# Normalizing and turning the attention heads by matmuls with diagonal blocks, in a fused linear-attention and ternary feed-forward kernel

## What is computed

```python
    S = S * jnp.exp(gt)[..., None, None]
    v_new = vt - jnp.einsum('bhk,bhkv->bhv', kt, S)
    S = S + bt[..., None, None] * (kt[..., :, None] * v_new[..., None, :])
    o = jnp.einsum('bhk,bhkv->bhv', qt, S)
...
var = jnp.mean(jnp.square(o.astype(jnp.float32)), axis=-1, keepdims=True)
o = o * jax.lax.rsqrt(var + NORM_EPS).astype(o.dtype) * norm_w
gate = (x @ Wg.T).reshape(B, T, H, DV)
o = o * jax.nn.silu(gate)
return o.reshape(B, T, H * DV) @ Wo.T
```

## Time and profile before

| what | value |
|---|---|
| median of 3 runs | 407.44 us (406.19 to 407.88) |
| the profiled execution: its time, its span | 409.17 us, 407.3 us |
| mean granted TensorE clock | 0.792 |
| DVE busy | 304.1 us, 75% |
| PE busy | 259.5 us, 64% |
| ACT busy | 119.9 us, 29% |
| chain that ended last | DVE 50%, PE 24%, issue 7%, ACT 4% |

### The profile page before, as it was taken

One profiled execution on the slowest core, in us unless ns is written; L12 is line 12 of the kernel. 1 busy time (PEld: TensorE's weight loads), 2 busy tenths in 40 slices (PEclk: granted clock), 3 DMA queues, 4 the chain that ended last, 5 costly groups with the idle time before them and its releaser, 6 DMA issues.

```text
span 407.3 us, 13992 instructions
## 1 busy us (share of the span) xinstructions
PE 259.5 (64%) x6314; PEld 177.6 (44%) x6314; DVE 304.1 (75%) x774; ACT 119.9 (29%) x245; POOL 32.5 (8%) x44
## 2 busy tenths in 40 slices
PE   3993650489558649696567659684484285986541
PEld 1492430445445417364443345353453264655321
DVE  0664898928689995949798987678899955438996
ACT  0783411046722210265413113347022001132010
POOL 2000110002201000011210000013010001010000
PEclk9965585569968868989689589897897595998686
DMA  8500000000000020000000030000000230001001
GB/s 242 208 0 2 2 2 0 3 3 3 3 2 3 3 51 3 2 3 2 3 3 2 4 103 3 2 3 2 4 3 2 63 96 2 3 3 53 2 1 52
DMA packets 8011, 9.65 MB, mean 24 GB/s; under 512 B 1808, under 2 KB 7056, under 8 KB 7952
## 3 DMA queue, kind: packets, MB, share of 16 engines
q1 hardware_dynamic: 7024, 8.41, 6.3%
q10 hardware_dynamic: 928, 0.36, 0.4%
HBM read 6.67 MB, written 2.10 MB: 22 GB/s over the span
## 4 chain that ended last, share of the span: by engine, by line
DVE 50%; PE 24%; issue 7%; ACT 4%; DVEq 0%
PE pc L329 6%; DVE conv_buf L894 4%; PE pj L342 4%; PE pg L450 3%; DVE inv L994 3%; DVE sub_buf L992 3%; PE fr L329 3%; PE fr L473 2%; PE pj L450 2%; DVE stats L1085 2%; DVE r_sb L1033 2%; DVE r_all L882 2%; DVE t_all L881 2%; DVE conv_buf L1079 2%; DVE t_all L880 2%
## 5 line engine op out<-in xcount | busy, mean ns | idle before, releaser
L894 DVE SCALAR_TENSOR_TENSOR conv_buf<-raw,wconv,conv_buf 128x512 f32<-128x512 f32 x72 | 57.6, 806 | 16.7 <-ACT conv_buf L616 15.0
L342 PE MATMUL pj<-xt,wproj 128*128 128x512 f32 x96 | 55.6, 718 | 7.8 <-DMA xt<-x_t 7.1
L684 ACT ACTIVATE u_sb<-pc 128x192 f32<-128x192 f32 x32 | 10.5, 328 | 107.2 <-PE pc L329 107.2
L329 PE MATMUL pc<-r_sb,t_t 32*32 32x64 f32 x672 | 17.1, 237 | 34.3 <-DVE r_sb L1033 33.5
L846 POOL TENSOR_TENSOR s_dec<-s_sb,decay 128x192 f32<-128x192 f32 x24 | 15.8, 660 | 282.5 <-DVE s_sb L1042 153.6
L342 PEld LDWEIGHTS pj<-xt,wproj 128*128 128x128 f32 x96 | 20.0, 228 | 27.6 <-issue 24.1
L329 PEld LDWEIGHTS pc<-r_sb,t_t 32*32 32x32 f32 x672 | 12.0, 115 | 44.8 <-DVE r_sb L1033 44.2
L329 PE MATMUL fr<-x_t,x 32*32 32x16 f32 x768 | 11.8, 210 | 30.5 <-DVE x_t L999 15.8
L329 PEld LDWEIGHTS fr<-x_t,x 32*32 32x32 f32 x768 | 11.2, 151 | 32.1 <-issue 32.1
L450 PE MATMUL pg<-wout,conv_buf 128*128 128x256 f32 x36 | 13.4, 547 | 17.9 <-DVE conv_buf L1079 17.9
L354 PE MATMUL pg<-xt,wproj 128*128 128x512 f32 x48 | 24.1, 624 | 0.0
(11 more groups left out here) (161 smaller groups left out, 534.3 us busy)
## 6 DMA issues: line engine op xcount, KB each, us to landing
xt<-x_t SPq DMA_DIRECT2D x1, 1536.0 KB, 9.1
x_buf<-x SPq DMA_DIRECT2D x3, 512.0 KB, 3.8
out<-hid_buf SPq DMA_DIRECT2D x6, 256.0 KB, 2.2
wproj<-w_proj SPq DMA_DIRECT2D x1, 1024.0 KB, 7.8
xt<-x_t SPq DMA_DIRECT2D x1, 512.0 KB, 5.8
kq<-x SPq DMA_DIRECT2D x1, 512.0 KB, 3.6
out<-v_tok SPq DMA_DIRECT2D x2, 256.0 KB, 2.1
wout<-w_out SPq DMA_DIRECT2D x1, 384.0 KB, 9.9
```

The source lines that it names most:

```text
L329: mm = pe.matmul(out[rows], stationary[rows], moving[rows], **flags)
L342: mm = pe.matmul(pj[:, j % 2, :], wproj[:, t, j * P:(j + 1) * P], xt[:, t, k * TOK:(k + 1) * TOK], start=(t == 0), stop=(t == KT - 1))
L684: act.activation(u_sb[:, :, :].rearrange("p g v -> p (g v)"), pc[:, 0:G3 * DV], ACT.Copy).then_inc(u_done, 1)
L894: e = dve.scalar_tensor_tensor(out=conv[:, d, :, :], in0=raw[:, d, :, m:m + T], scalar=wconv[:, j, m:m + 1], in1=conv[:, d, :, :], op0=ALU ...
```

## The change

- A constant `C_EYE` is added, a 32x32 identity repeated in each 32-row group.
- `head_norm` no longer scales `o_all` and no longer transposes. One DVE instruction writes `r_diag`, 24 diagonal 32x32 blocks with the reciprocal roots on the diagonal (128x768).
- PE's new `heads_to_channels(k)` stands after `merge(k + 1)`. For groups 0 and 1 it issues 2 x 2 x 8 calls of `by_head` (128 matmuls), for group 2 another 64 matmuls that go to off-diagonal blocks of the array. The results lie in four PSUM banks.
- `gated` reads them from PSUM, with four instructions in place of three, and waits for `turn_mm` in three steps.
- `project(k + 2, 0)` and ACT's `tile_out_of_psum(k + 2, 0)` move ahead of the junction's `merge`; the three taps of `conv_taps(…, 0)` move between the instructions of `gated`, for turns 0 and 1.
- `normalize` of the tail moves ahead of `gated`.
- `load_residual` waits for `r_diag_done` in place of `on_scaled`.

```diff
@@ constants
-C_UPPER, C_ROWA, C_ROWB, C_LESS_B, C_END = 644, 676, 677, 678, 679
+C_UPPER, C_ROWA, C_ROWB, C_LESS_B, C_EYE, C_END = 644, 676, 677, 678, 679, 711
...
+        r_diag = view(sub_buf, 0, U, CH)
...
+        head_bank = (pc[:, :], po[:, :], fr[:, 1, 0:T], pg[:, 0:T])
@@ SP
             def load_residual(k):
-                after(sp, on_scaled, 1, k, 1)
+                after(sp, r_diag_done, 1, k, 1)
@@ PE
+            def heads_to_channels(k):
+                after(pe, r_diag_done, 1, k, 1)
+                for h in range(2):
+                    for g in range(2):
+                        for c in range(NC):
+                            t = g * T + c * CH
+                            mm = by_head(head_bank[h][:, t:t + CH], o_all[:, g, c, h * 32:(h + 1) * 32],
+                                         r_diag[:, g * NC + c, :], start=True, stop=True)
+                    mm.then_inc(turn_mm, 1)
+                for c in range(NC):
+                    for h in range(2):
+                        for q in range(4):
+                            rows, at = slice(32 * q, 32 * q + 32), 64 * h + 32 * (q % 2)
+                            mm = pe.matmul(head_bank[2 + q // 2][at:at + 32, c * CH:(c + 1) * CH], o_all[rows, 2, c, h * 32:(h + 1) * 32],
+                                           r_diag[rows, 2 * NC + c, :], start=True, stop=True)
+                mm.then_inc(turn_mm, 1)
...
             def turn(k, front, tail):
-                if front and not first(k):
-                    project(k + 1, 0)
...
                 if front:
+                    if not last(k + 1):
+                        project(k + 2, 0)
                     merge(k + 1)
+                    heads_to_channels(k)
@@ ACT
                 merge_out(k)
-                if front and not first(k):
-                    tile_out_of_psum(k + 1, 0)
...
-                    after(act, on_done, 0, k, 1)
+                    after(act, turn_mm, 0, k, GATE_TILES)
...
                     o_square(k, front)
+                    if not last(k + 1):
+                        tile_out_of_psum(k + 2, 0)
@@ DVE
             def handoff(k, front, tail):
...
-                if front:
+                if front and first(k):
                     conv_taps(k + 1, 0)
...
-                units = o_all[:, :, :, :].rearrange("p g c v -> p (g c) v")
-                dve.tensor_tensor(units, units, r_o.unsqueeze(2).to_broadcast([P, U, DV]),
-                                  ALU.mult).then_inc(on_scaled, 1)
...
+                dve.tensor_tensor(r_diag, cst[:, C_EYE:C_EYE + CH].unsqueeze(1).to_broadcast([P, U, CH]),
+                                  r_o.unsqueeze(2).to_broadcast([P, U, CH]), ALU.mult).then_inc(r_diag_done, 1)
+
+            def gated(k, early):
+                after(dve, gate_done, GATE_TILES, k, GATE_TILES)
                 if not first(k):
                     after(dve, y_mm, 0, k, 2)
...
+                for j in range(2):
+                    after(dve, turn_mm, j + 1, k, GATE_TILES)
+                    dve.scalar_tensor_tensor(out=o_ch[:, j, :], in0=head_bank[j], scalar=nw[:, j:j + 1],
                                              in1=gate[:, j, :], op0=ALU.mult, op1=ALU.mult).then_inc(og_done, 1)
+                    if early:
+                        conv_tap(k + 2, 0, j)
+                after(dve, turn_mm, GATE_TILES, k, GATE_TILES)
+                for b in range(2):
+                    half = slice(b * T, (b + 1) * T)
+                    dve.scalar_tensor_tensor(out=o_ch[:, 2, half], in0=head_bank[2 + b], scalar=nw[:, 2:3],
+                                             in1=gate[:, 2, half], op0=ALU.mult, op1=ALU.mult).then_inc(og_done, 1)
+                if early:
+                    conv_tap(k + 2, 0, 2)
...
                     head_norm(k, tail)
-                    gated(k)
                     if tail:
                         normalize(hid, y_out, out_done)
+                    gated(k, not last(k + 1))
```

More of the change, by code:

```diff
@@ L242, in program @@
         gate_mm, gate_done = (sem(n) for n in ("gate_mm", "gate_done"))
[L243 to L244 removed]
+        osq_done, turn_mm, og_done, y_mm, y_in, xq_done, xqt_mm, xqt_done, ffn_mm, ffn_in, out_done = (
+            sem(n) for n in ("osq_done", "turn_mm", "og_done", "y_mm", "y_in", "xq_done", "xqt_mm",
                              "xqt_done", "ffn_mm", "ffn_in", "out_done"))
@@ L442, in to_state @@
                 mm.then_inc(o_mm, 1)
+            def heads_to_channels(k):
[14 more added lines that the diff above has]
+                mm.then_inc(turn_mm, 1)
             def project_out(k, part):
                 if part == 0:
-                    after(pe, og_done, GATE_TILES, k, GATE_TILES)
+                    after(pe, og_done, GATED, k, GATED)
                 for n in range(2 * part, 2 * part + 2):
@@ L654, in square @@
                 if not first(k):
-                    after(act, og_done, 0, k - 1, GATE_TILES)
+                    after(act, og_done, 0, k - 1, GATED)
                 act.activation(sq_tok[:, :, :, :, :].rearrange("p g k c d -> p (g k c d)"),
@@ L697, in gate_silu @@
                     if not first(k):
-                        after(act, og_done, 0, k, GATE_TILES)
+                        after(act, og_done, 0, k, GATED)
                     if not last(k):
@@ L888, in rsqrt, with conv_tap @@
                     rsqrt_newton(y, v, t)
+            def conv_tap(k, j, m):
+                if m == 0:
+                    after(dve, tile_out, j + 1, k, CONV_TILES)
+                d = SLOT[j]
+                e = dve.scalar_tensor_tensor(out=conv[:, d, :, :], in0=raw[:, d, :, m:m + T],
+                                             scalar=wconv[:, j, m:m + 1], in1=conv[:, d, :, :],
+                                             op0=ALU.mult, op1=ALU.add)
+                if m < TAPS - 2:
+                    own(e)
+                else:
+                    e.then_inc(conv_done[j], 1)
             def conv_taps(k, j):
[L891 removed]
                 for m in range(TAPS - 1):
[L893 to L900 removed]
+                    conv_tap(k, j, m)
             def kq_to_tokens(k):
```

33 lines of the change are left out of this document (4 added, 29 removed).

## The result

The changed kernel takes 425.83 us in the median of 4 runs (422.32 to 427.96), the kernel before beside it 407.56 us (406.19 to 407.88). The ratio is 1.042, with a 95% interval of 1.038 to 1.047. So 16.2 us of the gap of 18.3 us are in the two traces that are compared here.

A forecast was written before the change was run, and what follows sets the result against it. The prediction took the path from root to gated heads at three junctions as the bound. PE's waits for instruction blocks add 3.8, 4.9 and 5.6 us, +14.3 on 407.44, rounded to 421.5 us; own range 417 to 426, full range 409.5 to 427.

The forecast's parts named there:

- What bounds the kernel: At three junctions, 7.21 us from root to gated heads is on the path; DVE's work behind `gated` is worth nothing.
- Blocks of instructions: In the new matmuls, PE waits for blocks of 256 instructions, three a junction: +3.8, +4.9, +5.6 us at turns 0, 1, 2.
- Rival 1: Instruction blocks don't hold PE up in the new matmuls and the clock stays low: +1.0 us a junction, 410.5 us; chance 0.12.
- The signs that the prediction named: Groups of about 128 MATMUL, 1 to 2.5 us idle between, 8 to 11 us in all at turns 1 and 2.
- The time of a block: PE's next block of 256 instructions in a dense run takes 3.5 to 4.47 us, taken as 4.0.
- what is moved: Moved `project`, taps, ACT's copies, the residual's load (0.8 us earlier) and store (6 us earlier) are hidden: all zero.
- The products' own time: PE's 384 new MATMUL a junction take 15 ns each at the lower clock, 5.8 us, starting 1.05 us behind the root.
- rival 2: No block wait and PE's clock at full speed in products and `project_out` part 0: -2.4 us a junction, 400.2 us; chance 0.10.
- The moves at zero: At the junctions, the moved work falls into idle time or is covered by the wait for PE, so it costs zero.
- Behind `gated`: PE runs `project_out` part 0 (4.28 us), `merge_second` (1.72) and part 1 (2.80) as before.
- rival 3: The forecast's blocks, plus a low clock for `merge_second` and `project_out` part 1: +2.5 us a junction, 429 us; chance 0.11.
- DVE's transposes: At turn 1 DVE turns all heads in 3.35 us against 5.8 or more on PE; without block waits, a little lost.

The follow-up runs named there:

- experiment 2: The changed kernel with the residual's load, and the store queued behind it, waiting until PE has finished all products: 419.32 us, ratio 1.022.
- experiment 3: The changed kernel with 32 matmuls (128 PE instructions) of the first chunk products issued twice, far ahead of the junctions: one run, 432.99 us.
- experiment 4: The changed kernel with every second chunk's products left out and 64 columns each, so 384 instructions a junction in place of 768: 409.20 us, ratio 1.004.
- 10: The changed kernel with `project`, its two copies and the taps back in their old places, `normalize` still ahead of `gated`: 427.15 us, ratio 1.046.
- 5: The changed kernel with `project`, ACT's copies, the taps and `normalize` in their old places, so only the products on PE are new: 421.55 us, ratio 1.032.
- 9: The changed kernel with `normalize` back behind `gated`, so that the store leaves late: 422.61 us, ratio 1.036.
- 1: The changed kernel with all its moves, but DVE scaling and transposing the heads as before: 415.27 us, ratio 1.014.
- 6: The kernel before with only `project` and its two copies moved ahead of `merge`: 408.37 us, ratio 1.000.
- experiment 7: The kernel before with PE scaling and turning only group 2 while DVE does groups 0 and 1, no moves: 401.13 us, ratio 0.982.
- 8: The kernel of experiment 7 with `project` and its copies moved ahead of `merge`: 403.58 us, ratio 0.989.

## Why the prediction was right, point by point

**What bounds the kernel.** Right. Nothing outside the three junctions changed by more than 1.3 us, and DVE's 11.6 us less work did not make the kernel faster.

**Blocks of instructions.** Right, and shown by experiments 2, 3 and 4, not only argued. The sharpest is experiment 3, by which the holes move with the count of instructions. The places: at turn 1 block ends were forecast at instructions 224, 480 and 736. The holes stand at 478 and 734, twice 239 and 367. The first end shows none: its packet had started near 233.7 us, and the other holes end 2.2 to 2.9 us behind the start of theirs, so it was there at about 236.3 (an estimate), when PE came to it at 236.4. At turn 2, 428 and 684 were forecast and found (214 and 342 MATMUL). At turn 0 the count of the prediction gives 290 and 546 (34 and two blocks of 256) and the holes stand at 282 and 538, 8 instructions earlier. Rival 1, no block wait at 410.5 us, is out.

The Trainium skill (Runtime: NRT & Kernel Launch, "Instruction fetch mechanics") has the next 16 KB fetched while the present execute, at a cost that is mostly hidden. In the products this is not so: 256 instructions of this kind execute in about 2 us and the block takes 3.5 to 4, so it cannot be hidden.

The signs that the prediction named came, with two sizes off: groups of 128 MATMUL between holes, 11.1 and 12.0 us from first to last at turns 1 and 2 (8 to 11 were named) and 8.9 at turn 0, and first holes of 3.72 and 4.17 us (1 to 2.5 were named).

**The time of a block** was the term that was mis-sized, taken as 4.0 (3.5 to 4.47). Where no large transfer is in the way it is below that or at it: 152.11 - 148.38 = 3.73 us at turn 0, 3.46 us for the last block of turn 1 (241.97 to 245.43), 4.00 us at turn 2, 3.73 in experiment 2. Where 1 MB of data is in flight it is far above: at turn 1 PE entered the block that runs out at the hole 111 MATMUL into the products, at about 234.74 + 1.7 = 236.4, and the next came at 241.97, 5.5 us later; at turn 2, 86 MATMUL in, 328.3 to 334.25, 6.0 us. This is why the junctions read +3.67, +5.91 and +6.71 us where +3.8, +4.9 and +5.6 were forecast: right at turn 0, 1.0 and 1.1 us short at the others.

**The step that failed** in the prediction, although the time came out in its range, is in "what is moved": "The residual's load starts about 0.8 us earlier on SP's queue, the store about 6 us earlier against the gating; both were hidden." The times are right (the load leaves 0.99 us behind the root in place of 1.79, the store 1.63 us in place of 7.87), and they were hidden as data. They were not looked at as neighbours of the instructions on the same DMA engines. Moving both behind the products took 6.5 us off (experiment 2), of which the traces place 5.3 in the stretches up to `project_out`. The forecast was 4.3 us short. By size: with load and store in flight the first hole was 3.3 to 4.5 us at turns 1 and 2 (changed kernel, 10), with the load alone 2.1 to 2.4 (5, 9), with neither 1.5 to 1.7 (2). The 1.64 us in experiment 3, where the packet came first, shows that both in flight is not enough. The store without the load was not tried.

The measured 425.83 us lies at the very edge of the forecast's own range of 417 to 426, and that it lies inside is in part luck. By the prediction's own scale (+10 us with blocks of 3.5 us, +14.3 with 4.0) blocks of 3.7 us, as they are undisturbed, give about +12 (an estimate); the 4.0 hid about 2 us of the term that was left out. That 4.47 us a block gives 425.5 is chance as well: no block in the products took that time.

**The products' own time.** Right. 15 ns was taken and 15.1 measured; PE busy was forecast at 5.8 us and is 5.4 to 5.5. The start 1.05 us behind the root is 1.01. Off-diagonal blocks show no extra cost. They are fewer than the text ahead of the prediction says: by the kernel's indices a matmul of group 2 uses the rows from 32 q and the columns from `at`, and for half of them the two are the same, on the diagonal. At turn 0 the last 115 MATMUL, all of group 2, run from 152.11 to 153.53 us, 12 ns each. The lower clock was right: 0.50 in all three windows, so rival 2, at 400.2 us, is out. The reason given, that dense small matmuls don't raise it, does not hold for all runs: in experiment 2 at turn 2 the 128 MATMUL between the holes ran at 1.00 (1.28 us), and in experiment 4 at turn 2 the products, without a hole, had a mean of 0.64. At turn 1 the clock was in fact up shortly before, and then fell. Windows of the kernel after, over `project` and the first part of `merge`, then over the rest of `merge` behind its hole of 2.26 us:

```profile
225.30:230.30 5.00, 3.61 (x187) 2.26 (x180) 4.69 (x12) 2.99 (x4) 0.00 (x0) 1.00 0.02 5
232.60:234.70 2.10, 0.41 (x17) 0.30 (x16) 1.91 (x7) 0.49 (x1) 0.00 (x0) 0.50 0.04 8
```

`project` ahead of `merge` did raise the clock, as rival 2 had it, and the merge's first 175 MATMUL ran in 1.63 us in place of 2.63 for 180. The next block wasn't there, PE idled 2.26 us in place of 1.10, and the products began at 1.2 GHz. What the earlier clock gave was lost to the next hole.

**The moves at zero.** Right for DVE's and ACT's time and for the reason given, the wait for PE as cover (1, 6); uncovered, the moves cost 6.4 us in all (1). As a whole they were not at zero: with all of them undone the kernel is about 4 us faster (5: 1.032 for 1.042, and the intervals do not overlap). `normalize` ahead brings the early store (5.6 us between experiments 10 and 5), and `project` away from `project_out` costs it the higher clock, which about balances the time that it takes there (10).

**Behind `gated`.** "I leave it as it is", at 4.28 us, was a little short: 5.01, 4.93 and 4.50 us, where it was 4.84, 4.28 and 4.28. PE comes to it at 0.50, out of holes and 1.0 to 1.1 us of idle time, with no `project` between. The whole stretch grew by 1.0 us over three junctions, less than the 7.4 us of rival 3. `merge_second` kept the higher clock.

**The sum.** +14.3 us was forecast and +16.2 measured between the profiled executions. The executions of the changed kernel spread over 5.6 us (those of before over 1.7), so the median gap of 18.3 us has about 2 us that no trace here places. A spread of block times is a possible cause, but this was not measured.

**DVE's transposes.** The Trainium skill (VectorE: DVE Perf Modes, "Rules for kernel authors") has DVE as the fastest way for 32x32 transposes within a bank. The runs agree for the whole: 3.35 us, or 5.1 with the scaling that the products also do, against 5.4 us of PE work, or 9 to 12 us from the first to the last of them with the holes. For the choice in a kernel that is not all: with a third of it on PE beside DVE's two thirds, experiment 7, the kernel is 1.8% faster.

## What to carry to other kernels

Count instructions as well as cycles when work moves to TensorE: here 256 of its instructions came as one block of 16 KB, in 3.5 to 4 us undisturbed, so a dense run of small matmuls went at the pace of the blocks and not of the array. Look in the profile for holes named "issue" at equal counts of instructions, and keep large transfers out of such a run. An engine that is to help another does best with the part it can finish in the other's shadow, and a step that keeps TensorE at the higher clock ahead of a long matmul may be worth more than the gap it would fill elsewhere.

## What the runs showed that was not expected

- Instruction packets wait behind data on the DMA engines: a block took 5.5 to 6.0 us with 1 MB of load and store ahead of its packet, 3.5 to 4.0 without.
- A shift of 128 instructions far ahead of the junctions moved the time by 7 us (one run). A comparison of two orders of the same work can therefore carry a few us that belong to the places of the block ends.
- `project_out` part 0, 12 MATMUL of 256 columns, took from 2.75 to 5.49 us, by what TensorE did in the microseconds before it. With `project`, four MATMUL of 512 columns, directly ahead it took 2.75 to 2.94 us in experiments 5 and 10 and at turn 0 of 7, but 3.62 at turn 1 of 7. Behind the 384 small ones with their holes, or behind 2.5 us of idle time (8, turn 1), it took 4.5 to 5.5. Behind the products of experiment 4 at turn 2, which had no hole, it took 2.86, at a clock of 1.00 and without `project`. So the holes themselves are a likely part of the low clock; no experiment varied them alone.
- One point is open: the first root of turn 0 came at 143.65 us in the changed kernel and at 145.36 in experiment 2, with the same instructions up to there, and between 142.3 and 145.4 over all kernels but that of experiment 3. So about 2 us of the difference between two profiled executions can arise ahead of the junctions. No experiment asked why.
